# Macaron block with a selective scan: scanning each row by column halves, both channel groups in one unit

## What is computed

```python
x = x + 0.5 * ffn(layernorm(x))
x = x + ssm(layernorm(x))
x = x + 0.5 * ffn(layernorm(x))

def ffn(x):   # hidden width 768
    return (silu(x @ wg.T) * (x @ wu.T)) @ wd.T

def ssm(x):
    z, params = x @ W_z.T, x @ W_params.T
    dt = softplus(params[..., :64] @ W_dt.T + b_dt)
    u = silu(causal_conv4(x))
    A_tilde = exp(dt[..., None] * A)            # 16 states for each channel
    B_tilde = (A_tilde - 1) / A
    h[0] = B_tilde[0] * u[0]
    h[t+1] = A_tilde[t] * h[t] + B_tilde[t] * u[t]
    y = sum over n of C[t, n] * h[t, n] + u * D
    return (y * silu(z)) @ W_out.T
```

## Time and profile before

| | |
|---|---|
| median of three runs | 2578.41 us |
| profiled execution | 2578.04 us, of which the span from first to last instruction is 2576.0 us |
| granted TensorE clock, mean | 0.933 |
| DVE busy | 2287.3 us (89%), 2294 instructions |
| PE busy | 2290.1 us (89%), 9220 matmuls |
| POOL busy | 2074.4 us (81%) |
| ACT busy | 1984.9 us (77%), 257 table loads |
| first scan starts, last scan starts | 135.5 us, 2499.7 us |
| bytes moved by DMA | 307.97 MB |

### The profile page before, as it was taken

The page is one execution under the profiler, slowest core; times in us unless marked ns, Lnnn a source line. Parts: engine busy times, 40 slices in busy tenths (PEclk is TensorE's granted clock), DMA queues, the critical chain, the costliest instruction groups (busy, mean ns, idle before and its releaser), DMA issues.

```text
span 2576.0 us, 28487 instructions
## 1 busy us (share of the span) xinstructions
PE 2290.1 (89%) x9220; PEld 1382.1 (54%) x9220; DVE 2287.3 (89%) x2294; ACT 1984.9 (77%) x2830; POOL 2074.4 (81%) x1286
## 2 busy tenths in 40 slices
PE   6877799899998989999898999999899999988478
PEld 3443455556465555646555564655556565555245
DVE  2189999999999999999999999999999999999981
ACT  4668787887878788787877878787787878776643
POOL 2367988888798888879888888988888898888772
PEclk9887999999999999999999999999999999998689
DMA  2133334334343433434343343434334343433430
GB/s 73 34 118 120 131 116 130 128 118 139 108 147 116 131 130 117 139 108 147 121 132 121 119 139 107 148 121 133 122 119 139 107 147 122 133 114 115 140 115 17
DMA packets 112025, 307.97 MB, mean 120 GB/s; under 512 B 11201, under 2 KB 45314, under 8 KB 111874
## 3 DMA queue, kind: packets, MB, share of 16 engines
q1 hardware_dynamic: 111874, 306.13, 36.3%
HBM read 288.27 MB, written 17.83 MB: 119 GB/s over the span
## 4 chain that ended last, share of the span: by engine, by line
PE 50%; ACT 19%; DVE 13%; issue 10%; POOL 7%; DMA 1%; DVEq 0%; SPq 0%; POOLq 0%; ACTq 0%
PE work L543 19%; PE work L531 12%; DVE g_bank L977 7%; PE work L582 6%; ACT ring L781 5%; POOL acc L856 4%; PE work L511 4%; DVE ring L1008 4%; ACT normed L624 4%; PE work L553 2%; ACT L611 2%; PE work L560 2%; PE work L590 2%; ACT xt_lo L662 1%; PE work L597 1%
## 5 line engine op out<-in xcount | busy, mean ns | idle before, releaser
L856 POOL TENSOR_TENSOR acc<-acc,ring 128x1024 f32<-128x1024 f32 x512 | 1211.0, 2365 | 175.3 <-DVE ring L1008 154.8
L977 DVE TENSOR_TENSOR_SCAN g_bank<-du_bank,ring 128x1024 f32<-128x1024 f32 x512 | 1174.6, 2294 | 29.9 <-ACT du_bank L768 15.8
L543 PE MATMUL work<-wd_t,hid 128*128 128x256 f32 x3072 | 691.7, 386 | 22.2 <-DVE hid L948 18.5
L1008 DVE SCALAR_TENSOR_TENSOR ring<-g_bank,inv_a,ring 128x1024 f32<-128x1024 f32 x512 | 654.9, 1279 | 11.3
L543 PEld LDWEIGHTS work<-wd_t,hid 128*128 128x128 f32 x3072 | 596.3, 194 | 117.9 <-DVE hid L948 21.3
L781 ACT ACTIVATE ring<-dt,a_coef 128x1024 f32<-128x1024 f32 x512 | 548.0, 1138 | 1.5 <-DVE g_bank L977 0.2
L825 POOL TENSOR_TENSOR hid<-hid,sil 128x512 f32<-128x512 f32 x192 | 244.6, 1274 | 136.3 <-ACT hid L683 136.3
L531 PE MATMUL work<-xt_hi,wg_t 128*128 128x512 f16 x768 | 311.1, 405 | 42.7 <-ACT xt L649 15.7
L611 ACT ACT_TABLE_LOAD x257 | 329.7, 1283 | 4.6
L531 PE MATMUL work<-xt_lo,wg_t 128*128 128x512 f16 x768 | 310.8, 405 | 0.0
L531 PE MATMUL work<-xt_hi,wu_t 128*128 128x512 f16 x768 | 302.4, 394 | 5.3 <-ACT sil L675 5.2
(11 more groups left out here) (90 smaller groups left out, 2829.2 us busy)
## 6 DMA issues: line engine op xcount, KB each, us to landing
ring<-c_rows SPq DMA_DIRECT2D x512, 512.0 KB, 3.7
x_in<-L_attn_x SPq DMA_DIRECT2D x32, 512.0 KB, 4.6
out<-x_fin SPq DMA_DIRECT2D x32, 512.0 KB, 4.0
c_rows<-params SPq DMA_DIRECT2D x32, 32.0 KB, 3.4
ring<-L_ffn_w_gate SPq DMA_DIRECT2D x1, 768.0 KB, 5.8
ring<-L_ffn_w_up SPq DMA_DIRECT2D x1, 768.0 KB, 7.2
ring<-L_ffn_w_down SPq DMA_DIRECT2D x1, 768.0 KB, 10.5
wz_t<-L_attn_W_z SPq DMA_DIRECT2D x1, 256.0 KB
```

The costliest lines, as they stand in the source:

```text
L543: last = pe.matmul(dst[:, j * E:(j + 1) * E], hid[:, K.unit[f, bt, c, m] % HIDS, t:t + P], wd_t[:, m, :], start=(m == 0), stop=(m == HM - 1))
L856: nc.gpsimd.tensor_tensor(acc[bt % 2][:, h, :], acc[bt % 2][:, h, :], cg[:, slot, :], ALU.add).then_inc(S["summed"], 1)
L977: scan = nc.vector.tensor_tensor_scan(g_bank[:], du_bank[:], decay[:, a, :], 0.0, ALU.add, ALU.mult)
L1008: nc.vector.scalar_tensor_tensor(cg[:, k, :], g_bank[:], inv_a[:, h, s:s + 1], spread[:, k_c, :], ALU.mult, ALU.mult).then_inc(S["weighted ...
```

## The change

A unit becomes (state, column half) instead of (state, channel group). It covers both channel groups over 512 positions, so it has the same number of elements, and there are again 32 to a row: the 16 states of the first half, then the 16 of the second. The parts of a unit:

- DVE: two scans of 512 columns, one for each channel group, then two multiplications of 512 columns. Each has its own waits, so that a scan of group 0 only waits for the former multiplication of group 0. In the first half, one copy more takes the last column of both scans into `carry` (two numbers for each partition); in the second half a scan begins with that number (a pointer to one number per partition) in place of the constant 0.
- ACT: two exponentials of 512 columns for one of 1024.
- SP: the spread C row has 512 columns (256 KB for 512 KB), the count is unchanged.
- POOL: still one addition of 1024 elements, in two pieces of 512 for each partition; the same for `d` and `gate`.
- The first half of a row can start scanning once that half's softplus, convolution and accumulator start are there; `op` of a half waits for the gate of that half alone.
- `x_fin` takes the load of row 1 and `x_in` is the final buffer of the last row.
- `AT`, `PACE` and `LAG` give way to tables with a place of its own for each piece: `ROW` for a row in the middle, `HEAD` for row 0 and `TAIL` for row 15. Silu and exp pieces are no longer tied to a phase.

```diff
@@ tables (cut) and schedule()
-AT = {
-    "scan0": [0.67, -0.01], "cm": [0.75], "bc": [-4.95], "ld": [-57.56, -40.12], "ln1": [-41.46, -36.46],
...
+ROW = {
+    "gate": [17.601, 32.74],
+    "op": [35.195, 36.536, 36.943, 38.706],
...
+HEAD = {
+    "dt": [-11.719, 6.021, -6.803, 10.056],
...
+TAIL = {
+    "ln3": [22.29, 46.112],
+    "dn2": [43.475, 43.693, 77.289, 86.827],
+    "op": [22.146, 22.449, 39.817, 39.979],
...
+def paired(b):
+
+    return True
...
     for b in range(B):
+        seen = {}
+        for name, ev in row_events(b):
+            table = HEAD if b == 0 and name in HEAD else TAIL if b == B - 1 and name in TAIL else ROW
+            i = seen[name] = seen.get(name, -1) + 1
+            out.append((round(SLOTS * b + table[name][i], 3), len(out), ev))
     return [ev for _, _, ev in sorted(out)]
@@ SP
+                    t = slice(p * CH, (p + 1) * CH) if paired(bt) else slice(0, L)
...
-                    sp.dma_start(spread[:, k, :], c_rows[bt % 2, s:s + 1, :].to_broadcast([P, L])).then_inc(S[f"c_spread{k}"], 16)
+                    sp.dma_start(spread[:, k, 0:size],
+                                 c_rows[bt % 2, s:s + 1, t].to_broadcast([P, size])).then_inc(S[f"c_spread{k}"], 16)
@@ PE
-                    wait(pe, "gated", ("gate", bt, EH - 1))
+                    wait(pe, "gated", ("gate", bt, piece(bt, EH - 1, jp // 2)))
@@ ACT
-                    nc.scalar.activation(decay[:, slot, :], dt[bt % 2][:, h, 0:L], ACT.Exp,
-                                         scale=a_coef[:, h, s:s + 1]).then_inc(S["decay"], 1)
+                    for h in range(EH) if paired(bt) else (p,):
+                        dst, t = (halves(d)[:, h, :], slice(p * CH, (p + 1) * CH)) if paired(bt) else (d, slice(0, L))
+                        nc.scalar.activation(dst, dt[bt % 2][:, h, t], ACT.Exp,
+                                             scale=a_coef[:, h, s:s + 1]).then_inc(S["decay"], 1)
@@ POOL
-                    nc.gpsimd.tensor_tensor(acc[bt % 2][:, h, :], acc[bt % 2][:, h, :], cg[:, slot, :],
+                    v = part(bt, p, acc[bt % 2])
+                    nc.gpsimd.tensor_tensor(v, v, shaped(bt, cg[:, K.number[ev[1:]] % TERMS, :]),
                                             ALU.add).then_inc(S["summed"], 1)
@@ DVE, scan
-                        wait(dve, "weighted", earlier(ev, 1))
-                        wait(dve, "decay", ("ex",) + ev[1:])
...
-                        scan = nc.vector.tensor_tensor_scan(g_bank[:], du_bank[:], decay[:, a, :], 0.0, ALU.add, ALU.mult)
...
+                        if was and paired(was[1]) and was[3] == 0:
+                            wait(dve, "carried", was)
...
+                        for h in range(EH) if pair else (p,):
+                            less = EH - 1 - h if pair else 0
+                            wait(dve, "weighted", was, less=less if was and paired(was[1]) else 0)
+                            wait(dve, "decay", ("ex",) + ev[1:], less=less)
+                            g, du_h, d_h, v_h = (halves(x)[:, h, :] if pair else x for x in (g_bank[:], du_bank[:], d, v))
+                            first = [carry[:, k, s, h, :] if pair and p else 0.0 for k in range(2)]
+                            scan = nc.vector.tensor_tensor_scan(g, du_h, d_h, first[0], ALU.add, ALU.mult)
@@ DVE, cm
+                        for h in range(EH) if pair else (p,):
+                            wait(dve, "scanned", ("scan",) + ev[1:], less=EH - 1 - h if pair else 0)
...
+                            nc.vector.scalar_tensor_tensor(v, g, inv_a[:, h, s:s + 1], c_row,
+                                                           ALU.mult, ALU.mult).then_inc(S["weighted"], 1)
+                            if pair and p == 0 and h == 0:
+                                wait(dve, "scanned", ("scan",) + ev[1:])
+                                if not with_tiny:
+                                    nc.vector.tensor_copy(carry[:, 0, s, :, :],
+                                                          halves(g_bank[:])[:, :, CH - 1:CH]).then_inc(S["carried"], 1)
```

## The result

The changed kernel takes **2483.66 us** (median of four runs, 2481.45 to 2484.11), the kernel before beside it 2578.06 (2575.96 to 2578.85): a ratio of 0.9633, 95% interval 0.9617 to 0.965. The forecast was 2592 us with a range of 2525 to 2645.

What follows compares the result with a forecast made beforehand. DVE was taken to set the middle row, with time as head + DVE's work + DVE's waits + tail: 2576.0 - 25 - 22 + 7 + 79 - 25 = 2590 us, plus 2.0 around the span: 2592 us, range 2525 to 2645.

Steps and rivals of the forecast that it cites:

- Head and tail: Before the first scan and after the last multiplication: -25 us (first scan near 110) and -22 us (about 50 for 72.7).
- +79 for the unit: DVE's scans, multiplications and copy: 3.72 us a unit on average, 0.155 above 3.56, times 512 = +79 us.
- Two scans: 2.28: DVE, per unit: two 512-column scans take 2 x (2.205 - 1.067) = 2.28 us, without the pointer.
- two multiplications: 1.34: DVE, per unit: two 512-column multiplications with pointer scalars take 2 x 0.67 = 1.34 us.
- rival 2: On DVE, halves don't overlap: each 512-column instruction waits until the one before has drained, +322 us, 2835 us; 4%.
- rival 3: On DVE, the copy meets POOL and is held, 0.5 us in 256 units, +128 us, 2720 us; 5%.
- -25 of waits: DVE's waits inside the scan stretch: the 50 us it waits for PE should halve, -25 us; bounds -50 and +70.
- a middle row is set by DVE: Middle rows: DVE busy 144.4 us of a 150.3 us period and setting it, PE 4 us behind.
- Other engines: 0: ACT, POOL, SP and DMA: their changes add nothing to the time; ACT has 26 us free in a row, POOL 20.
- Bounds of its terms: 2565 to 2625: Whole kernel: span the stated bounds of the forecast's terms give around 2592 us.
- Rival 1, the ends win: Pointers free in the scan (+45 for +79), DVE never waits for PE (-50): 2533 us, reaching to 2575; 30%.
- 512 columns take 0.52: nothing added: ACT's exponentials: whole ones take about 1.04 us to the next start, 512 columns 0.52, so two halves add nothing.

Runs made afterwards that it cites:

- no_pointer: The changed kernel with the second half's scans starting from the constant 0.0, the carried state left out: 2482.01 us, ratio 0.9631 to the kernel before.
- The square of runs: Old or new order (without `HEAD` and `TAIL`) with whole units or halves: old 2578 (kernel before) and 2633 us, new 2611 and 2512 us.
- halves_wait_both: Changed kernel without `HEAD` and `TAIL`, `dt0` waiting for the softplus of both halves, last `dp` ahead of it: 2605.37 us, against 2511.57 with the wait for one half.
- light_act: The changed kernel with silu of z made for 64 of 512 columns from row 1 on: 2482.46 us, ratio 0.9634 to the kernel before.

## Why the prediction was wrong

The forecast put the span at 2590 us and it is 2479.7, 110 us less. In the sum's own terms 50 of these are collisions that it put at nothing, 37 the unit, 19 the waits and 4 the rest of DVE's list; the ends fit.

**Head and tail: right.** -24 and -23 us for -25 and -22. The first scan came at 111.6 (forecast 110) and 49.5 us lie behind the last multiplication (50).

**"+79 for the unit": right in sign, twice too large.** It measured +42: 3.652 us a unit for the 3.72 forecast, against 3.570 before (the forecast had 3.56). The terms that were off are the two pairs, and the kernel before by 5 us (1828.0 in the table for the 1823 added up). "Two scans: 2.28" measured 2.24 without a pointer, "two multiplications: 1.34" measured 1.30. Both were built with a fixed part of 0.07 us for each instruction, taken from the four-column row; in these pairs it is 0.05 (2.24 = 2 x (1.067 + 0.053)). The pointer's price was right: 0.06 a scan (1272 for 1212 ns) for "0.07", and 31 us in all when `no_pointer` took it away. The copy, "between 0.07 and 0.13; I take 0.07", measured 0.07. Rivals 2 and 3 are refuted by the same rows: the halves overlap, and the 256 copies took 17.1 us together, each 0.14 to 0.16 us long, 216 of them beside a running POOL instruction. On rival 2 the prediction left something out: the section of the Trainium skill that it cites (VectorE: DVE Perf Modes, "The DRAIN you can't avoid") also says that a next instruction that is not held starts earlier. The trace agrees: 1.12 us between two scans of 1.21.

**What was never priced: 50 us of collisions.** The earlier trace rows hold one of them, the `shift` of 0.56 us, and the text used it to price a danger (rival 3), not as a cost that the kernel before already paid. The second `ai` was read at 0.75 us from one row that nothing held and taken for all 64; the view by line has their median at 1148 ns. The square of runs puts 43 us of the 50 on the new places and 10 on the halves, near enough the sum. The traces show why the places matter: the second `ai` began beside a running POOL instruction 60 times of 64 before and 18 times now. Putting the `rm` and `ai` pieces back didn't undo it, so which places did it is open.

**"-25 of waits": right for PE, wrong for the rest.** The gaps fell by 44 us. The three waits for PE (`hid`, `acc`, the residual) went from 50.1 to 25.8 us, just as forecast. But the text let "the waits for POOL's rstd" keep their cause, and those 28.6 us are gone; small new ones took 9 back, decays and silus among them.

**The deeper fault: "a middle row is set by DVE".** The sum added DVE's work and DVE's waits as if they were independent. The experiments show that they are not. 33 us taken from DVE came back as 32 us of gaps (`no_pointer`); one wait of ACT for POOL, 5.6 us a row, made 90 us of DVE gaps without any DVE instruction changing (`halves_wait_both`, 130.2 for 40.8). In the new order halves have 28 us more DVE work than whole units with the late `dt0`, and 47 us fewer gaps. "Other engines: 0" looked at busy sums (ACT had 26 us free in a row) and not at what is queued behind a wait. The same finding limits the breakdown at the head of this section: it says where the time stood, and not that each part would have come off the time by itself.

**Where the gain came from.** A chain of runs adds up to it. From the kernel before to the new places of a middle row, still with whole units and their `dp` and `dt0` placed for them: -50 us (2527.17). To halves in these places: -16 (2511.57). To `HEAD` and `TAIL`: -28 (2483.66). So more than half of the gain is the order, the term that the forecast left at "the places are all new, though". Halves earn their part at the ends, where two rows of them and their tables take whole units from 2527.17 to 2491.68, and 8 to 16 us in the middle. There they need the first half's softplus alone, which lets the last `dp` stand at -1.165, behind `dt0`. A whole unit needs that `dp` ahead and pays for it by where `dt0` stands (2611 or 2527 us). It isn't a cost that the kernel before paid: its ACT waited 3.0 us at `dt0` in all.

**The bounds.** "Bounds of its terms: 2565 to 2625" doesn't follow from the terms: with each at its own low bound (unit -62, head -32, tail -28, waits -50) the sum is 2413 us, with each at its high one 2722. The time lies inside that and outside the range stated.

**Rival 1, the ends win,** came nearest (2533, 30%), yet by another route: pointers are not free, and the waits did not go to nothing. None of the rivals had the collisions of the kernel before.

**The exponentials: wrong, hidden.** "512 columns take 0.52: nothing added" came from instructions without a pointer scale. Four exponentials in the head take 2.56 us, the last 0.7 of it, so 0.61 to 0.63 us a piece; over the whole run the mean to the next start is 0.63 where nothing waits. On the page the exponentials are busy 112 us more (659.8 for the row below, of the kernel before) and the table loads 46 (375.9 for 329.7), of ACT's 134 in all; the rest of its list counts 24 less.

```profile
L781 ACT ACTIVATE ring<-dt,a_coef 128x1024 f32<-128x1024 f32 x512 | 548.0, 1138 | 1.5 <-DVE g_bank L977 0.2
```

ACT had room, and 18 us less of it changed the time by 1 us (`light_act`). The first decays of a row, though, are what a lighter DVE waits for (`no_pointer`).

**Right:** DVE's 3574 instructions, 293 table loads, nothing from the C rows.

## What to carry to other kernels

When a change comes with a new order of the work, run the new order with the old units too, and more than once: here it gave more than half of the gain, and the place of one piece moved that run by 84 us. Split the waits of a unit as you split the unit: what a half no longer needs at its start can be worth more than the instructions that the split adds (16 us here against 28 us more DVE work), but in an order laid for whole units it cost 55 us. Before adding up an engine's work, look at min, median and max of each line; a median far over the minimum is a cost already paid, which another order can give back. Where several engines are over 90% busy, don't treat work and waits as terms that add up: one can come back as the other. Look for the instruction at the head of an in-order list that waits for another engine.

## What the runs showed of the hardware

- A scan over 512 columns takes 1212 ns with a constant start and 1272 ns with a start from SBUF (1216 when the pointer is taken away). The next independent one starts 1.12 us after it.
- A copy of two numbers from PSUM takes 0.14 to 0.16 us and 0.07 to the next start, in all of 256 cases, 216 of them beside a running POOL instruction; a four-column instruction with two SBUF inputs takes 0.15 as well, but up to 1.84 us in the kernel before.
- A DVE instruction with two SBUF inputs that begins beside a POOL instruction of 512 or 1024 columns ends after it: where it is held, the 512-column one 0.54 to 0.55 us behind POOL's end, the four-column one 0.01 to 0.02 (54 and 39 cases in the kernel before, 17 and 8 after). Beside POOL's four-column `rstd` (1.02 us) the 512-column one kept its 0.75 us, seven times of seven.
- 1024-column broadcasts for 512-column ones, 134 MB more by DMA in 2.5 ms, changed no time (2483.4 for 2483.66 us).
- A change of ACT's table holds ACT for the 1.28 us of the load and some 0.03 us around it, here in the middle of the kernel after: the work before it ends at 1560.24, the exponentials start at 1561.55.

```profile
1559.64 0.60 ACT L815 ACTIVATE hid<-work 128x512 f32<-128x512 f32 x1 [0.27 <-PE work L663]
1560.25 1.28 ACT L743 ACT_TABLE_LOAD   x1
1561.55 3.79 ACT L921 ACTIVATE ring<-dt,a_coef 128x512 f32<-128x512 f32 x6
```
